# Two graph-convolution edge stages: the node-table product ahead of the gathers, the gathered rows added by VectorE, in place of identity products on TensorE

## What is computed

```
def _cgconv(x, edge_index, Wf, bf, Ws, bs):
    j, i = (edge_index[0], edge_index[1])
    z = jnp.concatenate([x[i], x[j]], axis=-1)
    m = jax.nn.sigmoid(z @ Wf + bf) * jax.nn.softplus(z @ Ws + bs)
    agg = jax.ops.segment_sum(m, i, num_segments=x.shape[0])
    return x + agg
```

## Time and profile before

| | us |
|---|---|
| three runs | 10926.67, 10941.0, 10946.07 (median 10941.0) |
| the profiled execution | 10924.85, its span 10923.1 |
| first edge stage, first to last gather | 256.8 to 2734.9 |
| second edge stage, first to last gather | 2803.2 to 5284.2 |
| the two GAT edge stages, first to last gather | 5408.8 to 7901.0, 8162.5 to 10673.5 |
| busy in the span: PE, DVE, ACT, POOL | 6133.0, 3780.2, 1828.7, 6747.6 |

### The profile page before, as it was taken

How to read it: one execution, slowest core, us unless ns; L and a number is a source line. 1 busy time by engine, 2 the same in 40 slices (tenths; PEclk the granted TensorE clock), 3 DMA queues, 4 the chain that set the end, 5 groups by cost and what they waited for, 6 DMA issues and landing times. The chain is left out here.

```text
span 10923.1 us, 113136 instructions
## 1 busy us (share of the span) xinstructions
PE 6133.0 (56%) x30283; PEld 4722.4 (43%) x30284; DVE 3780.2 (35%) x5844; ACT 1828.7 (17%) x2603; POOL 6747.6 (62%) x6802
## 2 busy tenths in 40 slices
PE   2777777777777777777413444444471344444446
PEld 1555555555555555555303333333350333333335
DVE  6333333333333333333402323223250222332226
ACT  1333333333333333333200000000010000000000
POOL 2666666666566666666366666666606666666661
PEclk6777777777777777777555555555555555555555
DMA  4222222222222222222322212222112221222221
GB/s 138 65 65 66 67 66 66 67 66 63 77 65 66 65 66 67 66 66 66 69 49 43 45 42 45 44 44 45 39 21 48 44 45 42 43 44 45 43 43 26
DMA packets 436626, 612.01 MB, mean 56 GB/s; under 512 B 180134, under 2 KB 217754, under 8 KB 434779
## 3 DMA queue, kind: packets, MB, share of 16 engines
q0 software_dynamic: 214032, 332.71, 13.7%
q1 hardware_dynamic: 217116, 262.20, 8.3%
q10 hardware_dynamic: 5193, 13.44, 0.4%
HBM read 575.04 MB, written 32.78 MB: 56 GB/s over the span
## 5 line engine op out<-in xcount | busy, mean ns | idle before, releaser
L706 POOL DMA_INDIRECT big<-q_table,idx_stage x3328 | 3309.7, 995 | 1592.7 <-issue 957.9
L1166 POOL DMA_INDIRECT big<-xl_table,idx_stage x3328 | 3336.2, 1002 | 1524.1 <-issue 1018.9
L1434 PE MATMUL bank<-msg,onehot 128*128 128x66 f32 x6656 | 1603.1, 410 | 1025.8 <-issue 974.9
L1434 PEld LDWEIGHTS bank<-msg,onehot 128*128 128x128 f32 x6656 | 1510.3, 325 | 1196.2 <-issue 1194.7
L801 PEld LDWEIGHTS bank<-big,wide 128*128 128x128 f32 x6656 | 1243.0, 263 | 1451.8 <-issue 1450.4
L801 PE MATMUL bank<-big,wide 128*128 x6656 | 1289.8, 351 | 774.3 <-DVE wide L737 495.3
L797 PE MATMUL bank<-big,ident 128*128 128x512 f32 x1664 | 1261.6, 846 | 172.9 <-DMA big<-q_table,idx_stage 93.0
L815 PE MATMUL bank<-msg,onehot 128*128 128x67 f32 (+1 forms) x6656 | 1156.7, 324 | 313.2 <-issue 213.5
L815 PEld LDWEIGHTS bank<-msg,onehot 128*128 128x128 f32 x6656 | 1073.9, 241 | 450.7 <-issue 448.9
L1284 DVE TENSOR_TENSOR wide<-wide,bank 128x528 f32 x416 | 293.0, 704 | 2457.6 <-DMA work<-in_dst 896.8
L587 DVE TENSOR_TENSOR onehot<-iota,dst_rel 128x1024 f32<-128x1024 f32 x832 | 1014.9, 1220 | 0.0
(11 more groups left out here) (226 smaller groups left out, 3515.3 us busy)
## 6 DMA issues: line engine op xcount, KB each, us to landing
wide<-rel_rows SPq DMA_DIRECT2D x416, 256.0 KB
big<-rel_rows SPq DMA_DIRECT2D x416, 256.0 KB
big<-q_table,idx_stage POOLq DMA_INDIRECT x3328
big<-xl_table,idx_stage POOLq DMA_INDIRECT x3328
q_table<-wide SPq DMA_DIRECT2D x12, 1024.0 KB, 5.1
edge_rows<-big SPq DMA_DIRECT2D x25, 257.0 KB, 6.4
xl_table<-big SPq DMA_DIRECT2D x12, 520.0 KB, 6.6
big<-in_edge_attr ACTq DMA_DIRECT2D x6, 1024.0 KB
```

The lines of the kernel that those rows point to most:

```text
L706: pool.indirect_dma_start(out=ring[:, group % UNROLL, s % GROUP, :], out_offset=None, in_=k.q_table, in_offset=bass.IndirectOffsetOnAxis(a ...
L1166: pool.indirect_dma_start(out=buf[p][:, s, :], out_offset=None, in_=k.xl_table, in_offset=bass.IndirectOffsetOnAxis(ap=k.idx_stage[:, s:s ...
L1434: nc.tensor.matmul(sums_of[j][:, ds(slots[i], C + 2)], onehot[j][:, i, :], msg[j][:, i, 0:C + 2], start=False, stop=False)
```

## The change

- `form` becomes one stage of a whole unit without gathered rows: eight products one-hot x `p_tab` block into PSUM (`near`), started and stopped each by itself. It waits for `s_Z` of unit c-2 (the place in PSUM) and for `s_T`. The identity product is gone.
- A new VectorE stage `land(c)`: it waits for the rows of both groups of unit c and for `s_X` of unit c, and adds PSUM and gathered rows into a buffer in SBUF, `pre` (1,024 columns); it signals `s_Z`.
- POOL waits once per unit (before step 0 of 8) for `s_Z` of the unit that had the place, in place of once per group for TensorE.
- ScalarE and the two `softs` read `pre` from SBUF in place of PSUM. ScalarE waits for `s_Z`.
- Lags: VectorE's slot u is now add(u-4), onehot_t(u), land(u-1), spread(u-2), softs(u-2), message(u-2). TensorE's slot u is form(u), segment_sum(u-3).

```
                 for s in range(P):
                     group = s // GROUP
-                    if s % GROUP == 0:
-                        wait(pool, (s_X0, s_X)[group % 2], b * BUNITS + ((group - UNROLL) // 2 + 1))
+                    if s % UNIT == 0:
+                        wait(pool, s_Z, b * BUNITS + (s // UNIT - 1))
                         pool.sem_inc(s_turn, 1)
...
+                def land(c):
+                    j = c % SETS
+                    for half in range(2):
+                        u = 2 * j + half
+                        v.wait_ge(s_row[u], gathered + (16 * GROUP * (c // SETS + 1) + row_base[u]))
+                    wait(v, s_X, n[c + 1])
+                    nc.vector.tensor_tensor(pre[j], near[j], landed[:, j], ALU.add).then_inc(s_Z, 1)
...
-                    stages(u, first, last, (3, add), (1, spread), (0, onehot_t), (1, softs), (1, message))
+                    stages(u, first, last, (4, add), (0, onehot_t), (1, land), (2, spread), (2, softs), (2, message))
...
-                    wait(act, s_X, n[c + 1])
+                    wait(act, s_Z, n[c + 1])
...
-                    pe.wait_ge(s_row[u], gathered + (16 * GROUP * (c // SETS + 1) + row_base[u]))
-                    if half == 0:
-                        wait(pe, s_softs, n[c - 1])
-                    nc.tensor.matmul(k.psum[u][:, :], k.ident[:, :], ring[:, u].rearrange("p i c -> p (i c)"), start=True, stop=False)
...
+                def form(c):
+                    j = c % SETS
+                    blocks = load_offsets(k, pe, TAB_ROW, it * (CG_UNROLL * UNIT) + c * UNIT, UNIT, (NB - 1) * 2 * C)
+                    wait(pe, s_Z, n[c - 1])
+                    wait(pe, s_T, n[c + 1])
+                    for i in range(UNIT):
+                        last_one = nc.tensor.matmul(near[j][:, i, :], turned[j][:, i, :],
+                                                    p_tab[:, ds(blocks[i], 2 * C)], start=True, stop=True)
+                    last_one.then_inc(s_X, 1)
...
-                    stages(u, first, last, (0, lambda c: form(c, 0)), (2, lambda c: segment_sum(c, 1)),
-                           (0, lambda c: form(c, 1)), (1, lambda c: segment_sum(c, 0)))
+                    stages(u, first, last, (0, form), (3, segment_sum))
```

More of the change, by code:

```diff
@@ L655, in cg_edges @@
     n = f"cge{layer}_"
-    (s_zero, s_S, s_T, s_X0, s_X, s_ln, s_softf, s_softs, s_sig, s_msg, s_agg, s_acc, s_idx, s_act) = (
-        k.sem(n + x) for x in ("zero", "onehot", "onehot_t", "pre_half", "pre", "ln", "soft_f", "soft_s", "sig", "msg", "agg", "acc", "idx", "act"))
+    (s_zero, s_S, s_T, s_X, s_Z, s_ln, s_softf, s_softs, s_sig, s_msg, s_agg, s_acc, s_idx, s_act) = (
+        k.sem(n + x) for x in ("zero", "onehot", "onehot_t", "near", "pre", "ln", "soft_f", "soft_s", "sig", "msg", "agg", "acc", "idx", "act"))
     s_row, row_base = k.rows, list(k.row_base)
@@ L662, in cg_edges @@
     p_tab = k.big[:, 0:NB * 2 * C]
-    ring = k.big[:, NB * 2 * C:NB * 2 * C + RING].rearrange("p (u i c) -> p u i c", u=UNROLL, c=2 * C)
+    ring_words = k.big[:, NB * 2 * C:NB * 2 * C + RING]
+    ring = ring_words.rearrange("p (u i c) -> p u i c", u=UNROLL, c=2 * C)
+    landed = ring_words.rearrange("p (j i c) -> p j i c", j=SETS, c=2 * C)
     acc = k.wide[:, NB * C:NB * (C + AW)]
@@ L668, in cg_edges @@
     soft = by_set(k.work[:, 0:UNROLL * GROUP * P].rearrange("p (u i c) -> p u i c", u=UNROLL, c=2 * C))
+    at += UNROLL * GROUP * P
+    pre = by_set(k.wide[:, at:at + UNROLL * GROUP * P].rearrange("p (u i c) -> p u i c", u=UNROLL, c=2 * C))
     onehot, msg = by_set(k.onehot), by_set(k.msg)
-    pre = [k.pairs[j][:, :, :].rearrange("p u (i c) -> p (u i) c", c=2 * C) for j in range(SETS)]
+    near = [k.pairs[j][:, :, :].rearrange("p u (i c) -> p (u i) c", c=2 * C) for j in range(SETS)]
     agg = [k.pairs[SETS + j][:, :, :].rearrange("p u c -> p (u c)") for j in range(SETS)]
@@ L720, in iteration @@
             def iteration(it, first, last):
-                n = counts(v, it * CG_UNROLL, -3, 3)
+                n = counts(v, it * CG_UNROLL, -4, 3)
+                gathered = it * (CG_UNROLL // SETS * 16 * GROUP)
                 def add(c):
@@ L805, in segment_sum @@
-                def segment_sum(c, half):
-                    j = c % SETS
[L807 to L811, removed]
-                    slots = load_offsets(k, pe, SPAN_ROW, it * (CG_UNROLL * UNIT) + c * UNIT + half * GROUP, GROUP, (UNIT - 1) * P)
-                    for i in range(GROUP):
-                        s = half * GROUP + i
-                        nc.tensor.matmul(agg[j][:, ds(slots[i], width)], onehot[j][:, s, :],
-                                                    msg[j][:, s, 0:width], start=False, stop=False)
-                    if half:
-                        close_span(nc, k, k.pairs[SETS + j]).then_inc(s_agg, 1)
+                n = counts(pe, it * CG_UNROLL, -3, 4)
@@ new lines, in segment_sum @@
+                def segment_sum(c):
+                    j = c % SETS
+                    slots = load_offsets(k, pe, SPAN_ROW, it * (CG_UNROLL * UNIT) + c * UNIT, UNIT, (UNIT - 1) * P)
+                    wait(pe, s_acc, n[c])
+                    open_span(nc, k, k.pairs[SETS + j])
+                    wait(pe, s_msg, n[c + 1])
+                    wait(pe, s_S, n[c + 1])
+                    for i in range(UNIT):
+                        nc.tensor.matmul(agg[j][:, ds(slots[i], width)], onehot[j][:, i, :],
+                                         msg[j][:, i, 0:width], start=False, stop=False)
+                    close_span(nc, k, k.pairs[SETS + j]).then_inc(s_agg, 1)
```

13 lines of the change are left out of this document (removed).

## The result

The changed kernel takes 11,231.1 us in the median of 4 runs (11,221.4 to 11,262.6), beside 10,943.5 us of the kernel before measured with it: a ratio of **1.027, 95% interval 1.0255 to 1.0283**, slower by 288 us where 524 us were forecast. The profiled execution took 11,239.5 us.

What follows compares the result with a forecast made beforehand. POOL's chain of gathers was taken to bound both stages. 220 waits of 5.2 us replacing 623 us give +521, with ends +526, on 10,925 us; with 16 us to the median it said 11,465 us, range 10,600 to 11,950.

Steps and rivals of the forecast that it cites:

- POOL's chain sets the end of both stages: Both changed edge stages: POOL's gathers, 2,078 us per stage undisturbed, set the end; only POOL's waits can be won or lost.
- I take the lateness as a property of these stages: Edge stages: PE's signals arrive late while gathers stream, many only when POOL goes quiet; cause not visible in the trace.
- The longer answer through Vector: POOL's wait: the late signal must pass add, onehot_t and land, 2.7 us more, so 5.2 us instead of 2.50.
- The number of waits: POOL in both changed stages: 220 waits, one in 1.9 units, bounded by 126 and 416.
- The softs read SBUF instead of PSUM: 0: VectorE's softs: moving their input costs nothing, at most 38 us for both stages, judged by POOL's busy time in GAT stages.
- Ends, +5 us: Stage ends: a pipeline one unit deeper adds about 2.5 us per stage, +5 us.
- Identity products removed, 0: PE: 1,260 us less busy time in all is worth nothing, as POOL never waits for PE's throughput.
- The sum: Whole kernel: 1,144 us of waits replace 623, +526 us with the ends, giving 11,465 us, 4.8% slower.
- PE's busy time falling by 1,200 us or more: Sign that the forecast is right, in the changed kernel's profile: PE's busy time falls that much and its clock does not rise.
- No longer late: Rival: with less PE work its signals stop being late, waits go; 10,320 us at full price, likelier 10,630; chance 0.26.
- The debt at 1.49 us per gather: Rival: gathers drain at that rate whatever holds them, so both stages stay, 10,925 to 10,965 us; chance 0.14.
- One wait per unit: Rival: every closing product's signal hangs until POOL is quiet, 416 waits of 5.2 us, +1,540 us, 12,480 us; chance 0.08.

Runs made afterwards that it cites:

- e8: Kernel before, with POOL asking once per unit of eight gathers instead of once per half unit: 9,660.4 us beside 9,662.9 us on a prompt chip.
- e1: The change with VectorE's slot reordered, onehot_t and land ahead of the add: 11,262.8 us, ratio 1.030 to the kernel before, on a late chip.
- e2: Kernel before, with both softs reading a constant stretch of SBUF instead of PSUM: 10,932.7 us, ratio 1.0004, on a late chip.
- e3: The change with two identity products per unit put back on PE, on constant data: 11,275.3 us, ratio 1.032 to the kernel before, on a late chip.
- e9: The change itself, unaltered, on a prompt chip: 9,551.6 us beside 9,658.6 us of the kernel before, ratio 0.989.
- e6: Kernel before, with only one gather in four in the first two edge stages: 7,918.5 us, ratio 0.820, on a prompt chip.
- e5: The change with land adding a constant stretch, gathered rows unused, POOL waiting only for its own rows: 9,891.3 us, ratio 1.024 to the kernel before, prompt chip.
- e4: Kernel before, with onehot_t moved ahead of the add in VectorE's slot: 10,899.1 us, ratio 0.997, on a late chip.

## Why the prediction was right, and where not

**POOL's chain sets the end of both stages: right**, on both kinds of chip. On the prompt ones nothing else is left of it.

**"I take the lateness as a property of these stages": wrong, and the step that mattered most.** It is a property of the chip, or of its condition in that hour. The kernel before is some 1,280 us faster where PE's signals arrive at once, and every one of the four edge stages has its part in that, GAT's included (2,492 and 2,511 us against 2,192 and 2,191 us in e8). The four stages' near equal length, which I took as a sign of a debt, is gone there as well.

**The longer answer through Vector: right in mechanism and size.** Forecast 2.7 us more per wait and 1.2 us for land; measured 2.57 us and 1.213 us. A wait of 5.2 us was forecast; by the table of waits 5.57 us came out, over all pauses 5.04 us. In e1 the answer falls to 2.0 us in 70 pauses, where only land stands in the way.

**The number of waits: mis-sized.** Forecast 220, measured 126 by name, or 165 pauses against 263 when counted. Before, most runs of gathers between two pauses were 12 or 16 long; after, 16, 24 or 32. With a longer answer more signals come home in one pause, and POOL then runs further. My lower bound of 126 waits was the count that came, by luck: the GAT stages' count, doubled. In place of +521 us, idle time grew by 155 us.

**"The softs read SBUF instead of PSUM: 0", bounded by 38 us: wrong**; the gathers grew by 147 us. Looking for this in the GAT stages' sum was too coarse. The kernel before had the test in it: gathers beside L587, which has two SBUF inputs, against gathers beside L743, which has one. How much of the 147 us the time really paid is open: in e2 the waits gave back 60 of 71 us.

**Ends, +5 us**: the pause between the two stages went from 68.3 to 77.0 us. **Identity products removed, 0**: by e3 they and their clock would add some 50 us. **The sum** as written adds up to 11,467 us, not 11,465. **PE's busy time falling by 1,200 us or more**: it fell by 570 us, as the table's products went from 351 to 425 ns and those of the segment sum from 324 to 380 ns at the lower clock.

**The rivals.** "No longer late" did come true, but on other chips and not by the change; there the change is faster, by shorter gathers and not by fewer waits. Its own sign of being wrong, Vector idle before land with the rows as releaser, is what e9 shows. The debt at 1.49 us per gather is no property of gathers: they go at 1.29 us in e9 and 1.32 us in e8. On a late chip it was not refuted. "One wait per unit" did not come, though its clock did: the two stages fell to 0.55 and 0.54. The Trainium skill's rule (TensorE: Matmul & The Clock Gate, HAM oscillation), that bursts of matmuls with waits between them leave the engine at half clock, fits these traces, 0.99 in e6 without such waits. But e3 has the clock back and is no faster.

The forecast of 4.8% came out at 2.7%: the right sign and the right mechanism on the chip it was made for, a count too high, and one cost missed. Part of the closeness is luck. The waits, forecast at +521 us, gave 155 us; the gathers' own length, put at nothing, gave nearly as much again. That the kernel ran on a late chip was luck too: on a prompt one the sign is the other.

## What to carry to other kernels

When a wait's releaser is called remote and its signal comes microseconds after the record that sends it, the trace may show the chip and not the kernel: run it on another chip before tuning against it, since here the sign of the change turns with it (+2.7% and -1.1%). Check such a signal by its receiver too, since events can be missing from the trace. Where signals are late, keep the instruction that frees the gathering engine directly behind the signal; where they are prompt, only the gather's own length counts. Before moving a Vector operand from PSUM to SBUF, compare gathers beside instructions with one and with two SBUF inputs, each form of instruction by itself.

## What the hardware showed that I had not expected

Of the chips met, one (and that of the first measurement) delivered PE's signals 3.4 us late in the median and up to 18.4 us late in the kernel before (first measurement, first stage); four delivered all that have an event within 0.3 us, the median within 0.01 us. Vector's signals to PE and ScalarE were prompt on the late chip. The same program took 10,935 and 9,652 to 9,663 us. In the kernel before on the late chip, both stages, 73 to 97% of the signals were on time when their product ended during the first four gathers after a pause of POOL; from the eighth gather on, 0 to 3%. What holds them back no run here shows.

A single gather beside two Vector instructions with two SBUF inputs each took 1.97 us instead of 0.94 us. And of two kernels in which POOL waits for nobody, the one whose Vector waits for the gathered rows was the faster (e9, 2,151 us a stage, against e5, 2,324 us).

No version was seen to beat both kernels on both kinds of chip. On a late one the fastest is e4, 0.3% under the kernel before (it was not run on a prompt one); on a prompt one it is the change as it is, 1.1% under it.
